# Second attention: both score passes through three shared slots of two PSUM banks, one VectorE maximum per two heads, the maxima copied by ScalarE beside the queries

## What is computed

```
# 32 heads in 8 groups of 4 that share one key/value head, head size 8
fused = x @ w_qkv.T + b_qkv
q = fused[..., :256]; k = fused[..., 256:320]; v = fused[..., 320:]
q -> (B, 8 groups, 4 heads, 512, 8);  k, v -> (B, 8, 512, 8)
sim  = einsum('bgrsd,bgtd->bgrst', q, k) / sqrt(8)
attn = softmax(sim, axis=-1)
out  = einsum('bgrst,bgtd->bgrsd', attn, v)
return out.reshape(B, 512, 256) @ w_out.T + b_out
```

## Time and profile before

| | |
|---|---|
| median of 3 runs | 1140.63 us (1138.54 to 1140.98) |
| span of the profiled execution (first to last instruction) | 1136.1 us |
| PE busy | 1018.1 us, 90% |
| VectorE busy | 762.7 us, 67% |
| ScalarE busy | 604.8 us, 53% |
| mean granted TensorE clock | 0.968 |

### The profile page before, as it was taken

One profiled execution on the slowest core, in us unless ns is written; L12 is line 12 of the kernel. 1 busy time (PEld: TensorE's weight loads), 2 busy tenths in 40 slices (PEclk: granted clock), 3 DMA queues, 4 the chain that ended last, 5 costly groups with the idle time before them and its releaser, 6 DMA issues.

```text
span 1136.1 us, 17535 instructions
## 1 busy us (share of the span) xinstructions
PE 1018.1 (90%) x5780; PEld 743.6 (65%) x5780; DVE 762.7 (67%) x1591; ACT 604.8 (53%) x911; POOL 317.4 (28%) x331
## 2 busy tenths in 40 slices
PE   4998898779999846799999999999999997999995
PEld 3877776669999724555555555555555565888884
DVE  6576454556655346798899888888888846444437
ACT  6325445355565543466665666666666665444431
POOL 2005777066655500000000122222221000455441
PEclk9999999989999967899999999999999998999999
DMA  6863333354444272011111222222222124333253
GB/s 231 315 263 126 124 110 120 113 195 150 136 124 135 89 305 35 14 28 29 29 29 29 43 55 57 56 56 57 56 56 43 63 73 155 108 108 101 92 196 137
DMA packets 49140, 120.49 MB, mean 106 GB/s; under 512 B 7752, under 2 KB 24904, under 8 KB 48520
## 3 DMA queue, kind: packets, MB, share of 16 engines
q1 hardware_dynamic: 36096, 82.80, 25.5%
q0 software_dynamic: 11808, 32.37, 7.5%
q10 hardware_dynamic: 1152, 4.19, 0.9%
HBM read 72.30 MB, written 52.42 MB: 110 GB/s over the span
## 4 chain that ended last, share of the span: by engine, by line
PE 65%; DVE 16%; POOL 7%; issue 4%; ACT 3%; DMA 3%; SPq 0%; ACTq 0%; DVEq 0%; POOLq 0%
PE psum L817 11%; PE psum L838 9%; PE psum L826 7%; DVE work_f L1699 6%; POOL xg L466 5%; PE psum L633 5%; PE psum L634 4%; PE psum L635 4%; PE psum L547 3%; PE psum L548 3%; PE psum L549 3%; PE psum L619 3%; PE psum L644 2%; DVE x L1310 1%; PE psum L665 1%
## 5 line engine op out<-in xcount | busy, mean ns | idle before, releaser
L1699 DVE TENSOR_REDUCE work_f<-psum 128x1 f32<-128x512 f32 x512 | 337.3, 685 | 49.1 <-PE psum L817 46.7
L1203 ACT ACTIVATE work_f<-psum 128x1024 f32<-128x1024 f32 x172 | 169.5, 1023 | 104.9 <-PE psum L826 100.5
L817 PE MATMUL psum<-work_r 128*128 128x512 f32 x512 | 207.8, 445 | 18.9 <-DVE work_f L1699 7.0
L473 POOL DMA_INDIRECT yk<-yb,dest x134 | 131.3, 980 | 240.1 <-ACT yb L1057 206.7
L817 PEld LDWEIGHTS psum<-work_r 128*128 128x128 f32 x512 | 93.4, 190 | 133.8 <-DVE work_f L1699 71.2
L826 PE MATMUL psum<-qm,work_r 128*128 128x512 f32 x512 | 160.8, 396 | 0.9 <-ACT work_f L1203 0.8
L466 POOL DMA_INDIRECT xg<-xn,slot x112 | 108.2, 966 | 180.9 <-PE psum L853 143.5
L826 PEld LDWEIGHTS psum<-qm,work_r 128*128 128x128 f32 x512 | 93.8, 188 | 24.1 <-ACT work_f L1203 6.2
L633 PE MATMUL psum<-wexp,xbh 128*128 x268 | 102.1, 381 | 7.4 <-issue 7.2
L1203 ACT ACTIVATE pt<-psum 128x1024 f32<-128x1024 f32 x84 | 82.8, 1022 | 45.9 <-PE psum L826 42.7
L634 PE MATMUL psum<-wexp,xbh 128*128 x268 | 96.4, 360 | 0.0
(11 more groups left out here) (218 smaller groups left out, 2065.2 us busy)
## 6 DMA issues: line engine op xcount, KB each, us to landing
xb<-xg SPq DMA_DIRECT2D x67, 258.0 KB
xg<-in_pad SPq DMA_DIRECT2D x1, 10320.0 KB
yg<-yk SPq DMA_DIRECT2D x20, 512.0 KB, 9.0
stage<-in_moe SPq DMA_DIRECT2D x16, 608.0 KB
xg<-in_pad SPq DMA_DIRECT2D x1, 7224.0 KB
work_r<-work_r SPq DMA_DIRECT2D x128, 48.0 KB
work_r<-work_r SPq DMA_DIRECT2D x32, 192.0 KB
stage<-in_moe SPq DMA_DIRECT2D x16, 384.0 KB, 3.7
```

The costliest lines, as they stand in the source:

```text
L473: nc.gpsimd.indirect_dma_start(yk[l], bass.IndirectOffsetOnAxis(ap=dest[:, j % 8, i:i + 1], axis=0), yb[l][:, j % 2, i, :], None).then_inc ...
L817: nc.tensor.matmul(next_bank(pe, ("scores", n), b_mx, n + 1), qs[g % 2][:, t * P:(t + 1) * P], km[g % 4][:, r, :], start=True, stop=True). ...
L1203: nc.scalar.activation(pt[((b * NG + g) * QT + t) % 3][:, 2 * h:2 * h + 2, :], psum[:, 3 + 2 * h:5 + 2 * h, :], ACT.Exp, scale=float(HD) * ...
L1699: v.reduce_max(mx[:, s % 2, i:i + 1], ring["scores", n], AX.X).then_inc(b_mx, 1)
```

## The change

- Both score passes take slots of two banks from one ring of three slots (`next_slot`, banks 0 to 5). A score step is now two matmuls (two heads) into one slot, and one VectorE maximum over both banks (128x1024 to 128x2). A unit has 8 score steps and 8 T pairs, 16 uses of slots.
- The ring's order is the program's: in the steady state T pair, score pair, T pair, score pair. A use waits until the use three before it is read, and that is one of the other kind: a score pair waits for an exponential, a T pair for a maximum.
- The transposed maxima, the transposed outputs and the projections go through one single bank (`small_bank`, bank 6), each waiting for the reading of the last.
- Queries have four buffers in place of two. The maxima are copied by ScalarE from bank 6 into rows 96 to 103 of the unit's query buffer (`maxima`), in place of VectorE's addition into `qm`. Scores use rows 0 to 95, T pairs rows 0 to 103.
- The pipeline is written over all 32 units as one sequence. The T pairs of unit u-1 begin at pair 3 of stage u and end at pair 2 of stage u+1 (`LAG = 3`); V groups stand at pairs 6, and 0, 2, 4 of the next stage.
- In stage 0 the order of layer norm pieces, first projections and scores is another.

The core of the diff (TensorE first, then ScalarE, then VectorE):

```
+        UNITS, PAIRS, LAG = B * NG, 2 * QT, 3
+        def next_slot(engine, use, reader, value):
+            n = len(emptied)
+            if n >= 2:
+                engine.wait_ge(*emptied[n - 2 if n < PAIRS else n - 3])
+            slots[use] = 2 * (n % 2 if n < PAIRS else (n - PAIRS + 2) % 3)
+            emptied.append((reader, value))
+            return slots[use]
...
-            def scores(b, g, i):
-                n = b * NP + g * QT * R + i
-                t, r = i // R, i % R
-                nc.tensor.matmul(next_bank(pe, ("scores", n), b_mx, n + 1), qs[g % 2][:, t * P:(t + 1) * P],
-                                 km[g % 4][:, r, :], start=True, stop=True).then_inc(b_sn, 1)
+            def scores(u, i):
+                t, h = i // 2, i % 2
+                bank = next_slot(pe, ("scores", u, i), b_mx, u * PAIRS + i + 1)
+                for r in range(2):
+                    ins = nc.tensor.matmul(psum[:, bank + r, :], qs[u % 4][0:24 * R, t * P:(t + 1) * P],
+                                           km[u % 4][0:24 * R, 2 * h + r, :], start=True, stop=True)
+                ins.then_inc(b_sn, 1)
+            def scores_t(u, i):
+                t, h = i // 2, i % 2
+                if i == 0:
+                    pe.wait_ge(b_qm, u + 1)
+                bank = next_slot(pe, ("scores_t", u, i), b_ex, u * PAIRS + i + 1)
...
+            def stage(u, early={}):
...
+                for i in range(PAIRS):
+                    if i < LAG and u >= 2:
+                        scores_t(u - 2, PAIRS - LAG + i)
+                    if i >= LAG and 1 <= u <= UNITS:
+                        scores_t(u - 1, i - LAG)
                     if front:
+                        scores(u, i)
+                    if i == 1 and 1 <= u <= UNITS:
+                        maxima_t(u - 1)
+                    if i % 2 == 0 and i < 6 and u >= 2:
+                        values(u - 2, 1 + i // 2)
+                    if i == 3 and projects(u) is not None:
+                        project(projects(u), u // NG + 1, small_bank(...))
...
+                    if i == 6 and 2 <= u <= UNITS:
+                        outputs_t(u - 2)
+                    if i == 6 and 1 <= u <= UNITS:
+                        values(u - 1, 0)
...
+            def maxima(u):
+                act.wait_ge(b_mt, u + 1)
+                rows = slice(24 * R, 26 * R)
+                copy(qs[u % 4][rows, :], psum[rows, SMALL, :]).then_inc(b_qm, 1)
...
-                        v.reduce_max(mx[:, s % 2, i:i + 1], ring["scores", n], AX.X).then_inc(b_mx, 1)
+                        v.reduce_max(mx[:, u % 2, 2 * i:2 * i + 2], psum[:, bank:bank + 2, :], AX.X).then_inc(b_mx, 1)
```

More of the change, by code:

```diff
@@ L190, in program @@
         mz = tr(QT, P)
-        qm_both = place("qm", on1 + 4104, [P, 2, S], f32r)
-        qm = [qm_both[:, n, :] for n in range(2)]
+        qs_more = place("qs_more", on1 + 4104, [P, 2, S], f32r)
+        qs += [qs_more[:, n, :] for n in range(2)]
         kv = tf(S)
@@ L284, in xt_bank, with projects, new_values, small_bank @@
         def xt_bank(layer, b, k):
[L287 to L309, removed]
+            return ((0, 2), (1, 3), (4, 5), (7, 4))[b][k] if layer == 1 else 2 * b + k
+        UNITS, PAIRS, LAG = B * NG, 2 * QT, 3
+        NEXT = {NG - 3: 0, NG - 2: 2, NG - 1: 1}
+        def projects(u):
+            return NEXT.get(u % NG) if u < UNITS - NG else None
+        def new_values(u):
+            return u % NG == 1 and NG < u < UNITS
+        slots, emptied = {}, []
+        def next_slot(engine, use, reader, value):
[5 more added lines that the diff above has]
+            return slots[use]
+        SMALL = 6
+        small_read = []
+        def small_bank(engine, reader, value):
+            if small_read:
+                engine.wait_ge(*small_read[-1])
+            small_read.append((reader, value))
+            return psum[:, SMALL, :]
         @block.sync
@@ new lines, in scores_t @@
+            def scores_t(u, i):
[3 more added lines that the diff above has]
+                bank = next_slot(pe, ("scores_t", u, i), b_ex, u * PAIRS + i + 1)
+                for r in range(2):
+                    ins = nc.tensor.matmul(psum[:, bank + r, :], km[u % 4][0:26 * R, 2 * h + r, t * P:(t + 1) * P],
+                                           qs[u % 4][0:26 * R, :], start=True, stop=True)
+                ins.then_inc(b_st, 1)
@@ L854, in maxima_t @@
                 ins.then_inc(b_mt, 1)
[L858 to L878, removed]
-                    if front:
[L880 to L899, removed]
-                        early[i]()
-                if not front:
-                    for i in range(QT * R):
-                        follow(b, s - 1, QT * R + i)
@@ L946, in _ @@
             pe.wait_ge(s_lc, 2)
[L947 to L951, removed]
+            for u in range(1, UNITS + 2):
+                stage(u)
             def attention_t(b):
@@ L1168, in compact @@
                 act.wait_ge(b_pj, b1 * 3 + (at + 1))
-                if not (isinstance(b1, int) and b1 == 0):
+                if b1:
                     if n < 2:
@@ L1182, in compact, with outputs @@
                     ins.then_inc(b_hi, 1)
[L1184 to L1187, removed]
+            def outputs(u):
+                act.wait_ge(b_pv, (u + 1) * QT)
+                if u >= 1:
+                    act.wait_ge(b_ox, u)
                 copy(ot[:], psum[:, 7, :]).then_inc(b_ot, 1)
[L1190 to L1193, removed]
-                        gating_exp(E1, 2, TT)
[L1195 to L1202, removed]
-                            nc.scalar.activation(pt[((b * NG + g) * QT + t) % 3][:, 2 * h:2 * h + 2, :], psum[:, 3 + 2 * h:5 + 2 * h, :],
-                                                 ACT.Exp, scale=float(HD) ** -0.5).then_inc(b_ex, 1)
-                    if t == 2 and following and NG - 3 <= s < NG:
-                        compact((0, 2, 1)[s - (NG - 3)], b + 1, ring["projection", b * 3 + s - (NG - 3) + 4], s - (NG - 3))
-                if last and s == NG:
-                    outputs(b, s - 1)
@@ new lines, in stage @@
+            def stage(u):
+                for i in range(PAIRS):
+                    if u == 2 and i == 2:
+                        gating_exp(E1, 2, TT)
+                    if i < LAG and u >= 2:
+                        exponentials(u - 2, PAIRS - LAG + i)
+                    if i >= LAG and 1 <= u <= UNITS:
+                        exponentials(u - 1, i - LAG)
+                    if i == 1 and 1 <= u <= UNITS:
+                        maxima(u - 1)
+                    if i == 4 and projects(u) is not None:
+                        compact(projects(u), u // NG + 1, psum[:, SMALL, :], u % NG - (NG - 3))
+                    if i == 4 and u >= 2:
+                        outputs(u - 2)
@@ L1217, in _ @@
             normalised(1, 2)
-            compact(1, 0, psum[:, 3, :], 2)
+            compact(1, 0, psum[:, SMALL, :], 2)
             high_parts(1, 2)
@@ L1674, in normalise, with stage @@
                                 ALU.mult).then_inc(b_on, 1)
-            def stage(b, s, last, early={}):
-                front, following = not (last and s == NG), not last and s >= 1
-                turn = turns(s, following)
-                first = isinstance(b, int) and b == 0
-                for i in range(QT * R):
+            def stage(u, early={}):
+                front = u < UNITS
+                for i in range(PAIRS):
+                    if 3 <= u < NG:
+                        next(to_mask1, None)
+                        next(to_mask1, None)
+                    if u == NG and i == 6:
+                        place_totals(1, psum[:, SMALL, :])
+                    if u == NG + 1:
+                        next(to_slots1, None)
+                        next(to_slots1, None)
+                    if i == 5 and projects(u) is not None:
+                        compact(projects(u), u // NG + 1, psum[:, SMALL, :], u % NG - (NG - 3))
+                    if front:
+                        bank = slots["scores", u, i]
+                        dve.wait_ge(b_sn, u * PAIRS + i + 1)
+                        v.reduce_max(mx[:, u % 2, 2 * i:2 * i + 2], psum[:, bank:bank + 2, :], AX.X).then_inc(b_mx, 1)
+                    if i == 4 and new_values(u):
+                        values_by_key(u // NG, psum[:, SMALL, :])
+                    if i == 6 and 2 <= u <= UNITS:
+                        normalise(u - 2, psum[:, SMALL, :])
@@ L1681, in stage @@
                     if i in early:
                         early[i]()
-                    if first and 3 <= s < NG:
-                        next(to_mask1, None)
-                    if routes(b, s) and i == 13:
-                        place_totals(1, ring["totals"])
-                    if first and s > NG:
-                        next(to_slots1, None)
-                    if i == turn["maxima"] + 1 and s >= 1:
-                        dve.wait_ge(b_mt, b * NG + s)
```

(2 more changed lines are left out.)

159 lines of the change are left out of this document (78 added, 81 removed).

## The result

The changed kernel takes 1171.16 us (1169.81 to 1171.91, 4 runs), the kernel before 1140.81 (1138.54 to 1141.4, 4 runs): ratio 1.0269, 95% interval 1.025 to 1.0287. It is slower by 30 us. The profiled spans are 1168.0 and 1136.1, 31.9 apart. The forecast was 1168, in 1146 to 1190.

A forecast was written before the change was run, and what follows sets the result against it. The prediction took TensorE to bound the kernel, VectorE second. Stages 2 to 31 at +1.13 each (+34), special stages -4, stages 0 and 1 -2, tail -1 gave +27 on 1140.6: 1168 us, range 1146 to 1190.

The forecast's parts named there:

- TensorE bounds the kernel; VectorE's load does not: Plain stage before: 12.75 of 13.23 us is TensorE's own work; removing all VectorE load brings at most 0.48.
- The reduction over two banks: VectorE's maximum over a two-bank slot: about 1.18 us, or 1.29 with no saving; either leaves VectorE below TensorE's sum.
- TensorE's floor: TensorE's plain stage without any wait: 13.10 us, with V groups in four separate spells at 1.20 each.
- Three waits of 0.42, at S4, S6 and S0: Score pairs 4, 6 and 0 of a plain stage each wait for an exponential to free their slot: 0.42 us each.
- A plain stage: Stage without projection or routing work: 14.36 us after the change against 13.23 before, +1.13 each.
- A projection changes nothing in that sum: Stages with a projection: its matmuls fill one score pair's wait (-0.42), another's grows (+0.6), so no difference from plain stages' +1.13.
- The stages after a projection: Three stages following those with a projection, with transposed values: extra over plain falls from +1.39 to about +0.5, -0.9 each.
- The routing stages: Stage with the routing steps, bound by VectorE: lightened by 1.5 us, it gives 1 more back.
- Stage 0 and 1: Start of the kernel, layer norm chain with less VectorE work in its way and an empty ring: -2 us (-5 to +3).
- Tail: End of the kernel, 16.10 us before: three slots rather than two places for the last exponentials, -1 us.
- The sum, +27: Whole kernel: +34 from stages 2 to 31, -4 special stages, -2 at the start, -1 at the end.
- the ring keeps up: Rival: TensorE finds each slot empty, plain stages stand at 13.10 us, kernel faster at about 1130; chance 0.12.

The follow-up runs named there:

- Half a maximum: Changed kernel with each maximum over the first 256 keys of both banks and exponentials at a hundredth of the scale: 1167.89 us, ratio 1.0219.
- ScalarE's copy alone: Kernel before with only four query buffers, maxima copied by ScalarE, scores on 96 rows and T pairs on 104: 1139.72 us, ratio 1.000.
- half exponential: Changed kernel with each exponential over one of its slot's two banks, two heads' values reading that half: 1135.26 us, ratio 0.9927.

## Why the prediction was right

- *TensorE bounds the kernel; VectorE's load does not.* Right. Half a maximum and ScalarE's copy alone both take load off VectorE, and neither shortens a plain stage.
- *The reduction over two banks takes 1.18, from the bounds 1.18 and 1.29.* It takes 1.223. The term had no effect, as the prediction had it.
- *TensorE's floor is 13.10 with four spells.* It is 13.16 with the waits taken away. The forecast had counted it from distances in one stage of the kernel before.
- *Three waits of 0.42, at S4, S6 and S0, for exponentials.* Right in place, cause and size: the chain passes through an exponential before exactly these, 0.43 each by the half exponential. The other S and T pairs lose nothing in plain stages. Only the idle time foreseen for their weight loads was too short: 0.61 to 0.62, not 0.3.
- *A plain stage 14.36, +1.13.* 14.45, +1.16 over the mean of those before.
- *A projection changes nothing in that sum.* Right: +1.14 for those nine stages, 1.13 foreseen. The two parts are there as well. S4 no longer waits, and S6 waits longer, 0.62 by the view in two of three stages and 1.20 in the third, where plain stages show 0.19: 0.43 and 1.01 more, 0.62 on average, 0.6 foreseen.

```profile
665.49 0.73 PE L828 MATMUL psum<-work_r 96*128 96x512 f32 x2 [0.62 <-ACT work_f L1197]
```

- *The stages after a projection give 0.9 back.* Right: +0.23 each. *The routing stages:* +2.06 in three, where I had about +1.5.
- *Stage 0 and 1: -2 (-5 to +3).* Not borne out, though inside its bounds: +2.1 up to the first transposed maxima and +0.3 in the next interval. The chain of the layer norm gained only 0.2 (its low parts end at 463.75, before at 463.98), and TensorE then waits for the values' copy: the logits start at 465.36, before at 464.03. Seven of the logits' 24 matmuls then run at the lower clock (granted 0.52 from 466.3 to 469.0, where before it was 1.00), and the 24 take 7.2 us, not 6.1. In the timeline after (a start every 0.43, not 0.23):

```profile
466.74 0.63 PE L560 MATMUL psum<-xt_hi,aw 128*128 128x512 f32 x1
467.17 0.63 PE L558 MATMUL psum<-xt_hi,aw 128*128 128x512 f32 x1
```

  In these two profiles that makes 1.3 of a later start and 1.1 of slower matmuls. Neither was tried in a run, and as the same code moves by 3 us and more up to there, even the sign of the term is not shown.
- *Tail -1.* The rows give -1.24 and +0.52 in the last interval, of a rest that varies by 2.5 between runs: no run shows this term, and its fit can be luck.

The sum, +27, came out at +30.4 between medians and +31.9 between spans. Of the 4.9 us missing between spans 4.4 are stage 0 and 1; the stages from 2 on gave +30.2 where +30 was foreseen.

The rival "the ring keeps up" is the useful one. It was refuted as the change stands, but not for three slots in any order: in another order of the same work the ring does keep up (13.32). In the changed kernel a slot came round after 1.49 where its turn was 1.84.
The Trainium skill advises rotating groups through PSUM banks (Perfetto Trace Analysis, Matmuls). By these runs that advice holds with a condition: the banks must come round no sooner than their turn.
The Trainium skill says that a change of tiling mode drains TensorE (TensorEngine Tiling (Array Packing), Key Properties). The 0.20 lost beside a single V group agrees with it, though no run here tells a drain from another cause.
The Trainium skill lists row modes of 128, 64 and 32 rows (TensorEngine Tiling (Array Packing), Available Configurations), and none that would part 96 rows from 104. The kernel before with these row counts, at a ratio of 1.000, agrees.

## What to carry to other kernels

For a ring of buffers, work out two numbers from a trace: the turn of a buffer (fill, consumer's start, consumer's work, release) and the producer's work until that buffer comes round again. Where the second is shorter the producer waits, however idle its consumer is on average; work that needs no buffer of the ring, put inside the run, is cover, and grouping it to save switches takes the cover away. Count on an engine's relief only as far as others wait for it in the stage that bounds: here 36 us of VectorE's work went and the kernel became 30 us slower.

## What was not expected of the hardware

- A VectorE maximum over two banks (128x1024) takes 1.223 us, one over 128x512 0.685 to 0.691, whether its 512 elements lie in one bank or, as 2 x 256, in two.
- ScalarE's copy of 8 partitions x 512 takes 0.577 us in the changed kernel, hardly less than one of 128 x 512 (0.586 to 0.589).
- Matmuls on 96 and on 104 rows alternate with a start every 0.23 us in the changed kernel, like those on 128 rows before.
